# Folding Wq and Wk ahead of the first transposes, one more gelu sum on GpSimd, and new instruction orders in a fused attention and routed-FFN block

## The chip, the cores and the metric

The kernel runs on one NeuronCore of a Trainium2 chip. The metric is device time in microseconds of one execution; lower is better. The kernel before takes 91.41 us, the median of three runs (91.35 to 91.45).

## The reference, cut to what is computed

The input x is 4 x 1024 x 128 in float32. Two sublayers follow each other, each with a layer norm in front and a residual around it.

```python
h = layernorm(x)
q, k, v = heads(h @ Wq + bq), heads(h @ Wk + bk), heads(h @ Wv + bv)   # 16 heads of 8
q, k = elu(q) + 1, elu(k) + 1
k = k / sqrt(sum(k * k) + 1e-6)
attn = (q @ k.T) @ v              # no softmax: computed as q @ (k.T @ v)
y = h + attn @ Wo + bo
x = x + layernorm(y) * gamma + beta
h = layernorm(x)
scores = h @ w_router             # the top 768 of 1024 tokens of each batch are selected
out = h, with gelu(h @ w_block) in the selected rows
x = x + out
```

## The kernel before

The 4096 tokens are 32 tiles of 128 rows. Four tiles make a half u (0 to 7); two halves make a batch b (0 to 3). Every half goes through the same stages, and the halves are interleaved by hand: each engine has one program, a plain list of calls such as `k_half(3)`, and it runs strictly in the order of the list. Engines wait for one another with semaphores. So the order of a list decides what stands behind a wait.

The stages, with the names used in the lists:

- **First norm.** VectorE (DVE) takes statistics (`first_stats`, `bn_x`), GpSimd (POOL) takes the inverse roots with a power operation (`first_roots`, `roots1`), and `normalise1` writes the normalised rows; halves 3 and 7 are normalised on ScalarE (ACT). TensorE (PE) transposes them (`first_transpose`, `transpose_h`), and ACT copies the transposes out of PSUM (`first_copy`, `copy_hT`).
- **Weights.** The biases and the centring of the normalised rows are folded into the weights by two products on PE in `fold_biases`, with `less_last` and `to_last`; `copy_w` (ACT) writes the result to `w_c`. `fold_back` does the like for the residual and bo, into `back`.
- **Queries and keys.** PE: `q_proj`, `k_proj` (`first_keys` for half 0). ACT: `exp_q_half`, `exp_k_half`. DVE: `q_half`, `k_half`. Then the norm of the keys: `square_k` (ACT), `key_sums` (DVE), `ln_norms`, `seed_norms`, `square_seed` (ACT), `key_norms` (DVE), `scale_k` (POOL).
- **Attention.** PE: `attention_matrix(b)`, `values(b)`, `attention_out(b)`, with `copy_hk` and `copy_M` on ACT and `mask_vk(b)` on DVE between them, and `y_half(u)`.
- **Second norm and residual.** `y_stats`, `variances2` (DVE), `roots2` (POOL), `scale_y` and `y_gamma` (DVE), `residual` (DVE; half 0 on POOL), and the statistics of the result, `x1_stats`, `variances3` (DVE), `roots3` (POOL), `affine3` (DVE: two instructions of 128x4).
- **Scores, gelu and merge.** PE: `transpose_x1`, `z_half`. ACT: `gelu`, `norm_sum`. `gelu_sum(u)` adds x1 to the gelu, 128x512; the string `GELU_SUM_BY` says for each half whether POOL or DVE does it. The rank of each token comes from eight comparisons a batch, `compare(b, J)` on DVE, masked by `mask_own`, and summed on PE; `drop_first` and `drop_last` make the flags and `merge(u)` (DVE) puts the rows together. SyncE (SP) stores them. The last half's second part goes out from ACT's queue.

PE starts with `BUSY` products of zeros, before any data has come, so that it is not idle ahead of the first real work. PSUM has eight banks, and `BANK_USES` lists, for each, which result takes it after which; `take` waits until the one before has been read out.

Lines that matter below: L751 `first_stats`, L764 `bn_x`, L773 `normalise1`, L779 `q_half`, L799 and L801 `key_norms`, L813 `mask_vk`, L833 `variances2`, L839 `variances3`, L846 and L847 `affine3`, L853 and L432 `gelu_sum` on DVE and POOL, L886 `residual`, L918 `compare`, L927 `mask_own`, L941 `merge`, L400 `scale_k`, L413 `roots2`, L426 `roots3`, L1152 the zeros, L1165 `first_transpose`, L1197 and L1199 `fold_biases`, L501 `copy_w`, L1174 `first_keys`, L1219 `k_proj`, L1252 `y_half`.

Of the kernel before, what the change touches and what calls it, by code (L numbers as in the profile page):

```python
# [12 lines left out]
P = 128  # L13
# [7 lines left out]
def preln_linear_attention_mod_ffn(nc, x, wq, bq, wk, bk, wv, bv, wo, bo, gamma, beta, w_router, w_block, out):  # L21
# [19 lines left out]
    GELU_SUM_BY = 'PPPPPDDD'  # L41
# [10 lines left out]
    with ExitStack() as ctx:  # L52
# [3 lines left out]
        def sem(name):  # L56
# [6 lines left out]
        hT = sb("hT", [P, U, HW])  # L63
# [40 lines left out]
        w_c = sb("w_c", [P, 3 * P])  # L104
# [11 lines left out]
        back = sb("back", [P, P])  # L116
# [11 lines left out]
        w_in, wo_in, wz_in = sem("w_in"), sem("wo_in"), sem("wz_in")  # L128
# [45 lines left out]
             ("sums", 6),),  # L174
            (("h", 1), ("k", 3), ("M", 0), ("y", 0), ("wz", 0), ("z", 1), ("z", 6), ("xt", 5), ("s", 4),
             ("sums", 3), ("ra", 1), ("ra", 2),),
            (("q", 0), ("q", 4), ("q", 7), ("xt", 1), ("y", 5), ("y", 6), ("sums", 1), ("xt", 7), ("z", 13),),
# [118 lines left out]
        BUSY = 14  # L296
# [29 lines left out]
        def _(pool):  # L326
# [123 lines left out]
            add_beta(3)  # L450
# [1058 lines left out]
```

## Time and profile before

| | us |
|---|---|
| median of the runs (lowest, highest) | 91.41 (91.35, 91.45) |
| the profiled execution | 91.51 |
| its span, first to last instruction | 89.8 |
| PE busy | 79.9 |
| DVE busy | 80.9 |
| ACT busy | 66.9 |
| POOL busy | 52.8 |

The span is what the trace shows. The profiled execution takes 1.71 us more than its span, which lies before the first and after the last instruction. Busy time counts overlapping instructions once; a row's own duration holds the fill and the drain of the engine's pipeline, so instructions that follow each other closely start earlier than the one before ends.

### The profile page before, as it was taken

The page shows a single profiled execution, that of the slowest core. Times are in us where ns is not written, and L with a number is a line of the kernel's source. Part 1 is how long each engine was busy: PE and PEld are TensorE (multiplying, and loading weights), DVE is VectorE, ACT ScalarE, POOL GpSimd, SP SyncE. Part 2 cuts the span into 40 slices and gives each one's busy share as a digit, 9 for nine tenths or more (in the row PEclk, how much of TensorE's full clock was granted, in tenths as well). Part 3 has the DMA queues.
Part 4 walks back from the last instruction along what each step waited for, and adds up shares of the span by engine and source line. Part 5 has one row for each costly group of instructions (what it writes and reads, how often), then busy time and mean ns, then how long its engine had stood idle before and what let it go on. Part 6 is the DMA issues. An engine that isn't in the chain of part 4 may idle for free.

```text
span 89.8 us, 2397 instructions
## 1 busy us (share of the span) xinstructions
PE 79.9 (89%) x816; PEld 68.4 (76%) x816; DVE 80.9 (90%) x258; ACT 66.9 (75%) x186; POOL 52.8 (59%) x79
## 2 busy tenths in 40 slices
PE   4998689999999999999999599999999797999700
PEld 1335656976797997999999599999998797779600
DVE  4368999999797897999999999999999999999960
ACT  5003599998999996753539799999799696998700
POOL 5265885989992997659770979769838400000000
PEclk9999999999999999999999999999999999999996
DMA  0899969970999999900000000000000000348456
GB/s 24 233 256 319 280 168 319 290 189 7 143 127 140 139 143 136 112 10 0 0 0 0 0 7 0 0 4 7 0 4 0 0 7 10 107 121 236 138 149 180
DMA packets 18113, 8.99 MB, mean 100 GB/s; under 512 B 819, under 2 KB 18102, under 8 KB 18102
## 3 DMA queue, kind: packets, MB, share of 16 engines
q1 hardware_dynamic: 13232, 6.49, 26.7%
q0 software_dynamic: 4160, 2.10, 21.5%
q10 hardware_dynamic: 710, 0.26, 1.1%
q8 instruction: 6, 0.10, 0.4%
q14 instruction: 5, 0.04, 0.1%
HBM read 4.66 MB, written 2.10 MB: 75 GB/s over the span
## 4 chain that ended last, share of the span: by engine, by line
PE 46%; DVE 41%; issue 4%; ACT 3%; DVEq 1%; POOL 1%; ACTq 0%
DVE beats L918 11%; PE bank L1219 7%; PE bank L1211 7%; PE bank L1152 6%; DVE xb_sb L886 5%; DVE x_sb L941 5%; DVE bn L893 4%; PE bank L1252 4%; PE bank L1228 4%; PE bank L1253 4%; PE bank L1188 3%; PE bank L1271 3%; DVE beats L927 2%; DVE bn L818 2%; DVE x_sb L853 2%
## 5 line engine op out<-in xcount | busy, mean ns | idle before, releaser
L918 DVE TENSOR_SCALAR beats<-s_row,s_col 128x1024 bf16<-128x1024 f32 (+7 forms) x32 | 15.5, 541 | 0.0
L595 ACT ACTIVATE norm_sb<-xb_sb,shift,gain 128x128 f32<-128x128 f32 x32 | 13.2, 507 | 2.7 <-DVE shift L847 2.7
L1252 PE MATMUL bank<-M_sb,qT 128*128 128x128 f32 x64 | 12.5, 277 | 0.0
L1253 PE MATMUL bank<-back,hT 128*128 128x128 f32 x64 | 12.4, 275 | 0.0
L413 POOL TENSOR_TENSOR r<-var,minus_half 128x4 f32<-128x4 f32 x8 | 8.1, 1025 | 5.8 <-DVE var L833 5.5
L400 POOL TENSOR_TENSOR k_sb<-k_sb,k_rnorm 128x512 f32<-128x512 f32 x8 | 9.3, 1252 | 2.7 <-DVE k_rnorm L801 2.7
L426 POOL TENSOR_TENSOR r<-var,minus_half 128x4 f32<-128x4 f32 x8 | 9.1, 1194 | 2.9 <-DVE var L839 2.9
L1252 PEld LDWEIGHTS bank<-M_sb,qT 128*128 128x128 f32 x64 | 9.7, 192 | 0.2 <-ACT M_sb L558 0.2
L1253 PEld LDWEIGHTS bank<-back,hT 128*128 128x128 f32 x64 | 9.7, 192 | 0.0
L588 ACT ACTIVATE x_sb<-bank,r 128x128 f32<-128x128 f32 x32 | 9.2, 383 | 0.2 <-DVE s_col L901 0.2
L1219 PEld LDWEIGHTS bank<-w_c,hT 128*128 128x128 f32 x56 | 6.9, 192 | 2.1 <-ACT hT L513 1.1
L1271 PE MATMUL bank<-wz_c,hT 128*128 128x129 f32 x64 | 8.5, 278 | 0.0
L1219 PE MATMUL bank<-w_c,hT 128*128 128x128 f32 x56 | 7.3, 277 | 0.9 <-ACT hT L513 0.9
L1211 PE MATMUL bank<-hT,w_c 128*128 128x512 f32 x16 | 8.0, 593 | 0.0
L1228 PE MATMUL bank<-k_sb,norm_sb 128*128 128x128 f32 x64 | 7.8, 275 | 0.0
L1271 PEld LDWEIGHTS bank<-wz_c,hT 128*128 128x128 f32 x64 | 7.7, 192 | 0.0
L886 DVE SCALAR_TENSOR_TENSOR xb_sb<-bank,r,xb_sb 128x128 f32<-128x128 f32 x28 | 7.6, 338 | 0.0
L1228 PEld LDWEIGHTS bank<-k_sb,norm_sb 128*128 128x128 f32 x64 | 7.5, 192 | 0.0
L1292 PE MATMUL bank<-ident,beats 128*128 128x128 bf16 x108 | 6.8, 219 | 0.6 <-DVE dropped L936 0.6
L394 POOL DMA_DIRECT2D xb_sb<-beta_sb x4 | 7.0, 2060 | 0.1
L1152 PE MATMUL bank<-idle 128*128 128x512 bf16 x14 | 5.8, 601 | 1.3 <-DVE idle L735 1.3
L1292 PEld LDWEIGHTS bank<-ident,beats 128*128 128x128 bf16 x108 | 6.2, 98 | 0.9 <-DVE beats L918 0.8
(132 smaller groups left out, 216.7 us busy)
## 6 DMA issues: line engine op xcount, KB each, us to landing
xb_sb<-in_L_attn_x_dram SPq DMA_DIRECT2D x4, 512.0 KB, 6.8
xb_sb<-beta_sb POOLq DMA_DIRECT2D x4, 512.0 KB, 8.4
x_sb<-in_L_attn_x_dram SPq DMA_DIRECT2D x7, 256.0 KB, 5.2
out_dram<-x_sb SPq DMA_DIRECT2D x7, 256.0 KB, 2.3
x_sb<-in_L_attn_x_dram SPq DMA_DIRECT2D x2, 128.0 KB, 2.7
out_dram<-x_sb SPq DMA_DIRECT2D x1, 128.0 KB, 2.4
out_dram<-x_sb ACTq DMA_DIRECT2D x1, 128.0 KB, 2.5
w_sb<-in_L_attn_Wq_dram ACTq DMA_DIRECT2D x1, 64.0 KB, 2.5
```

Source lines behind the costliest of these rows:

```text
L400: nc.gpsimd.tensor_tensor(out_keys, keys, norms, ALU.mult).then_inc(keys_pool, 1)
L595: last = nc.scalar.activation(norm_sb[:, t], xb_sb[:, t], ACT.Identity, bias=shift3[:, t:t + 1], scale=gain3[:, t:t + 1])
L886: last = nc.vector.scalar_tensor_tensor(out=xb_sb[:, n], in0=bank_of(("y", u))[:, t * P:(t + 1) * P], scalar=r2[:, n:n + 1], in1=xb_sb[:, ...
L918: nc.vector.tensor_scalar(beats[:, b % 2, J, P * J:T * P], s_row[:, b, P * J:T * P], s_J, None, ALU.is_le).then_inc(beats_done, 1)
L1152: nc.tensor.matmul(bank[:, 7, :], idle16[:, 0:P], idle16[:], start=True, stop=True)
L1211: nc.tensor.matmul(take(("q", u)), w_c[:, 0:P], hT[:, u], start=True, stop=True).then_inc(q_full, 1)
L1219: last = nc.tensor.matmul(o[:, t * P:(t + 1) * P], hT[:, u, t * P:(t + 1) * P], w_c[:, P:2 * P], start=True, stop=True)
L1228: last = nc.tensor.matmul(o[:, 0:P], norm_sb[:, T * b + t], k_sb[:, 2 * b + t // TH, t % TH], start=(t == 0), stop=(t == T - 1))
L1252: nc.tensor.matmul(o, qT[:, u, t * P:(t + 1) * P], M_sb[:, b], start=True, stop=False)
L1253: last = nc.tensor.matmul(o, hT[:, u, t * P:(t + 1) * P], back[:], start=False, stop=True)
L1271: last = nc.tensor.matmul(o[:, j * (P + 1):(j + 1) * (P + 1)], hT[:, u, t * P:(t + 1) * P], wz_c[:], start=True, stop=True)
L1292: last = nc.tensor.matmul(o[:, n * P:(n + 1) * P], beats[:, b % 2, J, I * P:(I + 1) * P], ident16[:], start=(I == J), stop=(I == T - 1))
```

## The change

- **Fold.** `fold_biases` folds only Wq and Wk (256 columns in place of 384), and stands in front of `first_transpose(0)`. It waits for two weights and two biases. Wv and its bias have semaphores of their own, `wv_in` and `bv_in`, and are folded by two products of 128 columns in `fold_back`. `back` holds both results, `copy_back` copies 256 columns, and `values` reads Wv from it and waits for it for batch 0.
- **Queues.** The load of Wv on SP's queue goes out behind the load of half 1 of x instead of ahead of it.
- **Zeros.** `BUSY` is 10 in place of 14.
- **Gelu sums.** `GELU_SUM_BY` gives `gelu_sum(5)` to POOL, which then has six of eight.
- **Orders.** The lists of POOL, ACT, DVE and PE and the table of banks are new. No operation other than those above is added or left out.

```diff
-    GELU_SUM_BY = 'PPPPPDDD'
+    GELU_SUM_BY = 'PPPPPPDD'
-        BUSY = 14
+        BUSY = 10
@@ sync
                         sp.dma_start(x_sb[:, t:t + TH // 2, :], x_v[b, :, t:t + TH // 2, :]).then_inc(x0_in[h], 16)
-                    sp.dma_start(w_sb[:, 2 * P:3 * P], wv).then_inc(w_in, 16)
                 else:
                     sp.dma_start(x_sb[:, TH * u:TH * u + TH, :], x_v[b, :, a:a + TH, :]).then_inc(x_in[u], 16)
+                if u == 1:
+                    sp.dma_start(w_sb[:, 2 * P:3 * P], wv).then_inc(wv_in, 16)
@@ gpsimd, the list from scale_k(4)
             scale_k(4)
             roots2(0)
             scale_k(5)
+            residual(0)
             roots2(1)
-            residual(0)
+            add_beta(3)
             scale_k(6)
-            scale_k(7)
+            roots3(0)
             roots2(2)
             roots2(3)
-            roots3(0)
             roots3(1)
+            scale_k(7)
             roots2(4)
+            roots3(2)
             roots2(5)
             gelu_sum(0)
             gelu_sum(1)
-            roots3(2)
             roots3(3)
             roots3(4)
             roots2(6)
...
             roots3(5)
             roots3(6)
+            roots3(7)
             gelu_sum(4)
-            roots3(7)
+            gelu_sum(5)
@@ scalar, the first calls
+            copy_w()
             first_copy(0)
-            copy_w()
             first_copy(1)
             exp_k_half(0)
+            exp_q_half(0)
             copy_hT(1)
+            square_k(0)
             normalise1(3)
-            square_k(0)
             exp_k_half(1)
             copy_hT(2)
-            exp_q_half(0)
             copy_hT(3)
@@ vector, the first calls
             normalise1(1)
+            k_half(0)
             bn_x(4)
+            shifts1(2)
             bn_x(5)
-            shifts1(2)
-            k_half(0)
             normalise1(2)
             bn_x(6)
             bn_x(7)
+            k_half(1)
             normalise1(4)
-            k_half(1)
-            normalise1(5)
+            q_half(0)
             key_sums(0)
             key_sums(1)
-            q_half(0)
+            shifts1(4)
+            normalise1(5)
+            k_half(2)
+            q_half(1)
             normalise1(6)
@@ vector, around batch 0's comparisons, the list after
             variances2(5)
             score_cols(1, 0)
             score_cols(1, 1)
             residual(4)
             affine3(1)
             y_gamma(5)
             affine3(2)
             x1_stats(4)
             variances3(3)
             mask_vk(3)
             residual(5)
             compare(0, 0, 1)
...
@@ vector, the end of batch 2's comparisons, the list after
             compare(2, 5, 1)
             drop_last(0)
             affine3(6)
             variances3(7)
             compare(2, 6, 1)
             compare(2, 7, 1)
             drop_first(1)
             mask_own(2, 1)
             gelu_sum(6)
             merge(0)
             affine3(7)
             drop_last(1)
             score_cols(7, 0)
             score_cols(7, 1)
             merge(1)
             merge(2)
             merge(3)
             compare(3, 4, 1)
...
@@ tensor
-                o = take(("wp", 0))[:, 0:3 * P]
-                nc.tensor.matmul(o, less_last[:], w_sb[:], start=True, stop=False)
-                pe.wait_ge(bias_in, 16 * 3)
-                nc.tensor.matmul(o, to_last[:], bias_rows[:], start=False, stop=True).then_inc(w_full, 1)
+                o = take(("wp", 0))[:, 0:2 * P]
+                nc.tensor.matmul(o, less_last[:], w_sb[:, 0:2 * P], start=True, stop=False)
+                pe.wait_ge(bias_in, 16 * 2)
+                nc.tensor.matmul(o, to_last[:], bias_rows[:, 0:2 * P], start=False, stop=True).then_inc(w_full, 1)
@@ fold_back
-                nc.tensor.matmul(take(("rp", 0))[:, 0:P], less_bo[:], centre[:], start=True, stop=True).then_inc(back_full, 1)
+                o = take(("rp", 0))
+                nc.tensor.matmul(o[:, 0:P], less_bo[:], centre[:], start=True, stop=True)
+                pe.wait_ge(wv_in, 16)
+                nc.tensor.matmul(o[:, P:2 * P], less_last[:], w_sb[:, 2 * P:3 * P], start=True, stop=False)
+                pe.wait_ge(bv_in, 16)
+                nc.tensor.matmul(o[:, P:2 * P], to_last[:], bias_rows[:, 2 * P:3 * P], start=False, stop=True).then_inc(back_full, 1)
@@ tensor, the first calls
             busy_start()
+            fold_biases()
             first_transpose(0)
-            fold_biases()
             first_transpose(1)
             first_keys(0)
             first_keys(1)
+            q_proj(0)
             transpose_h(1)
             k_proj(1)
-            q_proj(0)
+            q_proj(1)
             transpose_h(2)
             transpose_h(3)
-            q_proj(1)
-            transpose_h(4)
             k_proj(2)
             k_proj(3)
+            transpose_h(4)
+            q_proj(2)
+            q_proj(3)
+            q_proj(4)
             transpose_h(5)
-            q_proj(2)
+            fold_back()
             k_proj(4)
-            q_proj(3)
             k_proj(5)
```

## Rows read from the trace of the kernel before

**Rows 1.** The page, first part: busy time, share of the span, instructions.
```profile
PE 79.9 (89%) x816; PEld 68.4 (76%) x816; DVE 80.9 (90%) x258; ACT 66.9 (75%) x186; POOL 52.8 (59%) x79
```

**Rows 2.** DVE's timeline, its waits from 5.7 us on: start, duration, instruction, wait.
```profile
5.95 0.76 DVE L764 BATCH_NORM_STATS2 bn<-x_sb 128x6 f32<-128x256 f32 x2 [0.24 <-DMA x_sb<-in_L_attn_x_dram]
...
23.97 0.69 DVE L779 SCALAR_TENSOR_TENSOR qT<-exp_q,bank 128x512 f32<-128x512 f32 x1 [0.57 <-ACT exp_q L521]
...
27.63 0.29 DVE L813 TENSOR_TENSOR vk_sb<-bank,head_mask 128x128 f32<-128x128 f32 x1 [0.47 <-PE bank L1234]
...
31.22 0.29 DVE L799 SCALAR_TENSOR_TENSOR k_tmp<-k_ssq,k_tmp 128x128 f32<-128x128 f32 x1 [0.40 <-ACT k_tmp L550]
...
35.12 0.29 DVE L813 TENSOR_TENSOR vk_sb<-bank,head_mask 128x128 f32<-128x128 f32 x1 [0.49 <-PE bank L1234]
```

**Rows 3.** The timeline's end: DVE's last merges.
```profile
85.43 1.39 DVE L941 COPY_PREDICATED x_sb<-dropped,norm_sb 128x512 f32<-128x512 int32 x3
```

**Rows 4.** The timeline of the first 12 us: zeros, fold, first keys, SP's load.
```profile
1.26 5.76 PE L1152 MATMUL bank<-idle 128*128 128x512 bf16 x14 [1.26 <-DVE idle L735]
...
1.79 0.46 SPq L308 DMA_DIRECT2D w_sb<-in_L_attn_Wv_dram  x1
...
6.86 0.38 PE L1165 MATMUL bank<-ident,norm_sb 128*128 128x128 f32 x2
...
7.08 0.81 PE L1197 MATMUL bank<-w_sb,less_last 128*128 128x384 f32 x2
...
8.57 0.48 ACT L501 COPY w_c<-bank 128x384 f32<-128x384 f32 x1 [0.92 <-PE bank L1199]
...
8.89 1.10 DVE L773 TENSOR_SCALAR norm_sb<-x_sb,bn,r 128x127 f32<-128x127 f32 x4
...
11.64 1.16 PE L1219 MATMUL bank<-w_c,hT 128*128 128x128 f32 x8 [0.88 <-ACT hT L513]
```

**Rows 5.** The timeline: the normalisation of half 5, and the start of `y_half(0)`.
```profile
15.86 1.23 DVE L773 TENSOR_SCALAR norm_sb<-x_sb,bn,r 128x127 f32<-128x127 f32 x4
...
29.33 0.39 PE L1252 MATMUL bank<-M_sb,qT 128*128 128x128 f32 x2
```

**Rows 6.** Groups by line: busy time and mean duration of `gelu_sum` on DVE and POOL.
```profile
L853 DVE TENSOR_TENSOR x_sb<-x_sb,xb_sb 128x512 f32<-128x512 f32 x3 | 1.9, 673 | 0.0
...
L432 POOL TENSOR_TENSOR x_sb<-x_sb,xb_sb 128x512 f32<-128x512 f32 x5 | 6.5, 1302 | 0.5 <-ACT x_sb L588 0.5
```

**Rows 7.** The timeline and groups: DVE instructions beside long POOL instructions on SBUF.
```profile
32.95 0.32 DVE L833 TENSOR_SCALAR var<-y_sq 128x4 f32<-128x4 f32 x1
...
39.94 2.11 POOL L400 TENSOR_TENSOR k_sb<-k_sb,k_rnorm 128x512 f32<-128x512 f32 x2 [1.09 <-DVE k_rnorm L801]
...
41.30 0.76 DVE L833 TENSOR_SCALAR var<-y_sq 128x4 f32<-128x4 f32 x1
...
67.76 1.42 POOL L432 TENSOR_TENSOR x_sb<-x_sb,xb_sb 128x512 f32<-128x512 f32 x1
...
67.98 1.29 DVE L918 TENSOR_SCALAR beats<-s_row,s_col 128x128 bf16<-128x128 f32 x1
...
L833 DVE TENSOR_SCALAR var<-bn 128x4 f32<-128x4 f32 x4 | 0.5, 157 | 0.0
```

**Rows 8.** The timeline: a comparison beside a power operation of POOL.
```profile
54.21 1.08 POOL L426 TENSOR_TENSOR r<-var,minus_half 128x4 f32<-128x4 f32 x1
...
54.50 0.75 DVE L918 TENSOR_SCALAR beats<-s_row,s_col 128x1024 bf16<-128x1024 f32 x1
```

**Rows 9.** The timeline around `gelu_sum(0)`: roots on POOL, residuals and an affine on DVE.
```profile
49.28 1.98 POOL L413 TENSOR_TENSOR r<-var,minus_half 128x4 f32<-128x4 f32 x2 [2.70 <-DVE var L833]
...
50.63 2.15 DVE L886 SCALAR_TENSOR_TENSOR xb_sb<-bank,r,xb_sb 128x128 f32<-128x128 f32 x8
...
52.70 0.16 DVE L846 TENSOR_SCALAR gain<-r 128x4 f32<-128x4 f32 x1
...
52.99 1.28 POOL L432 TENSOR_TENSOR x_sb<-x_sb,xb_sb 128x512 f32<-128x512 f32 x1 [0.48 <-ACT x_sb L588]
```

More of the change, by code:

```diff
@@ L683, in _ @@
             copy_xT(3)
+            norm_sum(2)
+            gelu(2, 0)
+            y_stats(7)
+            copy_s_row(2)
             copy_xT(4)
-            norm_sum(2)
-            y_stats(7)
-            gelu(2, 0)
+            copy_xT(5)
             gelu(2, 1)
@@ L1026, in _ @@
             residual(3)
-            affine3(0)
+            x1_stats(2)
+            y_stats(4)
+            variances3(2)
+            variances2(4)
+            y_stats(5)
+            y_gamma(4)
             score_cols(0, 0)
-            y_stats(4)
-            x1_stats(2)
             x1_stats(3)
-            y_stats(5)
             score_cols(0, 1)
-            variances2(4)
             variances2(5)
@@ L1037, in _ @@
             score_cols(1, 1)
-            variances3(2)
-            y_gamma(4)
+            residual(4)
+            affine3(1)
             y_gamma(5)
-            residual(4)
+            affine3(2)
+            x1_stats(4)
+            variances3(3)
+            mask_vk(3)
             residual(5)
-            affine3(1)
-            mask_vk(3)
-            x1_stats(4)
-            x1_stats(5)
-            variances3(3)
-            variances3(4)
             compare(0, 0, 1)
@@ L1051, in _ @@
             compare(0, 2, 1)
-            affine3(2)
             compare(0, 3, 1)
+            variances3(4)
+            score_cols(2, 0)
+            mask_own(0, 0)
             compare(0, 4, 1)
             compare(0, 5, 1)
-            mask_own(0, 0)
-            variances3(5)
-            y_stats(6)
-            score_cols(2, 0)
-            variances2(6)
             score_cols(2, 1)
             compare(0, 6, 1)
+            affine3(3)
             compare(0, 7, 1)
+            y_stats(6)
+            x1_stats(5)
+            variances2(6)
+            mask_own(0, 1)
+            variances2(7)
             score_cols(3, 0)
-            variances2(7)
             y_gamma(6)
+            variances3(5)
+            y_gamma(7)
             score_cols(3, 1)
-            y_gamma(7)
-            mask_own(0, 1)
-            score_cols(4, 0)
-            score_cols(4, 1)
             residual(6)
@@ L1087, in _ @@
             compare(1, 7, 1)
-            x1_stats(7)
-            drop_last(0)
-            affine3(4)
-            variances3(7)
             score_cols(6, 0)
-            affine3(5)
-            affine3(6)
+            mask_own(1, 1)
             compare(2, 0, 1)
-            mask_own(1, 1)
             compare(2, 1, 1)
+            drop_first(0)
             compare(2, 2, 1)
             compare(2, 3, 1)
+            score_cols(6, 1)
             compare(2, 4, 1)
+            mask_own(2, 0)
             compare(2, 5, 1)
+            drop_last(0)
+            affine3(6)
+            variances3(7)
             compare(2, 6, 1)
             compare(2, 7, 1)
-            score_cols(6, 1)
-            drop_first(0)
+            drop_first(1)
+            mask_own(2, 1)
+            gelu_sum(6)
+            merge(0)
+            affine3(7)
+            drop_last(1)
             score_cols(7, 0)
             score_cols(7, 1)
-            merge(0)
-            mask_own(2, 0)
-            mask_own(2, 1)
-            drop_last(1)
-            gelu_sum(5)
-            drop_first(1)
+            merge(1)
+            merge(2)
+            merge(3)
             compare(3, 4, 1)
@@ L1252, in y_half @@
                     nc.tensor.matmul(o, qT[:, u, t * P:(t + 1) * P], M_sb[:, b], start=True, stop=False)
-                    last = nc.tensor.matmul(o, hT[:, u, t * P:(t + 1) * P], back[:], start=False, stop=True)
+                    last = nc.tensor.matmul(o, hT[:, u, t * P:(t + 1) * P], back[:, 0:P], start=False, stop=True)
                 last.then_inc(y_full, 1)
@@ L1399, in _ @@
             values(1)
+            centre_wz()
             q_proj(7)
@@ L1410, in _ @@
             y_half(4)
+            y_half(5)
+            transpose_x1(2)
             z_half(0, 0)
             z_half(0, 1)
-            y_half(5)
             z_half(1, 0)
```

225 lines of the change are left out of this document (107 added, 118 removed), and 24 rows, old and new, of the table BANK_USES.

## The prediction

> **What bounds the kernel now.** I read the page first. Its first part says that DVE is busy 80.9 us of 89.8, more than any other engine [rows 1]. PE is as good as level with it, 79.9 us, and shares of busy time do not tell who sets the end, so I went to DVE's timeline and listed its waits. After 5.95 us there are four, 0.57 us at 23.4, 0.47 at 27.2, 0.40 at 30.8 and 0.49 at 34.6, together 1.93 us; from 35.12 us to the last merge at 86.82 (85.43 + 1.39) DVE waits for nobody [rows 2, 3]. The reader is to see a queue that is simply full: between 5.95 and 86.82 lie 80.87 us, of which 1.93 are waits. What comes behind the last merge is a store. So a faster step on PE or ACT is worth something only where it takes away one of those four waits, and every instruction taken from DVE is worth its whole time.
>
> One more thing in DVE's time is not work. The last comparison of batch 1, 128 columns, lasts 1.29 us, beside a POOL `gelu_sum` from 67.76 to 69.18, and ends at 69.27, right behind it. `variances2` of 128x4 lasts 0.76 us at 41.30 beside the second of two `scale_k`, and ends at 42.06 when POOL's ends at 42.05; the same operation elsewhere has a mean of 157 ns [rows 7]. So some DVE instructions stand still until a long POOL instruction on SBUF is through. A power operation of POOL does not do that: a comparison of 1024 columns takes 0.75 us beside one [rows 8]. The stalls at 41.30 and 67.98 cost 0.60 and about 1.02 us (1.29 less some 0.27 for 128 columns, an estimate from 0.75 for 1024 and 0.16 for 4); a third, 0.32 us at 32.95, is 0.16 us over the mean [rows 7]. That makes 1.8 us in all.
>
> **The change, part by part.**
>
> *The gelu sum.* One 128x512 addition leaves DVE. Its mean is 673 ns, of which some 0.60 is start to start; POOL takes 1.30 us for it [rows 6] and is busy 52.8 us of 89.8 [rows 1]. Gain 0.60.
>
> *SP's queue.* Wv goes out behind half 1 of x. Its issue takes 0.46 us [rows 4], so half 1 can arrive up to that much earlier, and DVE waits for it 0.24 us [rows 2]. Bounds 0 and 0.24. Later waits for ACT and PE may eat part of it; I take half, 0.12.
>
> *Zeros and fold.* The fourteen zeros take 5.76 us from 1.26 us on, and the first transpose starts at 6.86 [rows 4]. That is 0.41 us for each, or nearly 512 columns at the 1.2 GHz level (0.427), though the column of the granted clock reads 1.00 there; the last one ran at 2.4 GHz, as do the two transposes and the fold at 7.08 (two instructions of 384 columns in 0.81 us, fill and drain included). So 13 x 0.427 + 0.21 = 5.76, and PE's clock rose near 6.5 us. With ten zeros PE is free at 1.26 + 10 x 0.427 = 5.5 us. The fold's first product of 256 columns then takes about 0.86 us at the low level (0.64 for 384 columns without the fill, times 256/384, times 2), the second ends at about 6.9. `copy_w` starts near 7.1 instead of 8.57, 1.5 us earlier. If PE stays at the low level for both products and the two transposes it is 7.5 instead. Neither reaches DVE: half 1 is normalised from 8.89 to 9.99 us because DVE has been busy since 5.95, and PE can't transpose it before. The gap that opens on PE takes `q_proj(0)`. `k_proj(1)`, at 11.64 us before because ACT had `exp_k_half(0)` ahead of the copy, moves to about 11.3 [rows 4]. Moving Wv's two products costs PE nothing in sum (2 x 128 columns later for 2 x 128 sooner). Gain of this part on the end: 0 by itself, 0.3 us of lead for PE; the bound above is the four waits, 1.93 us, the one below is no loss.
>
> *The front of the lists.* Here work is only moved. DVE now does `k_half(0)`, `k_half(1)`, `q_half(0)` and two key sums ahead of `normalise1(5)`, which moves from 15.86 us to about 18.0 [rows 5]. Behind it wait `transpose_h(5)`, `fold_back` and `k_proj(4)` in PE's list. I followed PE's list with the durations of before: it loses about 0.45 us waiting for `copy_hT(2)` and 0.4 for `scale_k(1)`, has done `q_proj(0)` early (0.87), carries 0.44 more of Wv, and comes to `y_half(0)` at 29.3 to 29.4 us, against 29.33 [rows 5]. So the lead is spent, and the train of y halves runs at its old times. DVE's waits move: the one for `exp_q` goes, but with `square_k(5)` late on ACT and `key_sums(5)` behind it the wait for the norms of batch 2 grows from 0.40 to about 1.0; `mask_vk(1)` has 0.45, `key_sums(5)` 0.25, `y_stats(3)` 0.2. That is 1.9 to 1.95 us against 1.93. Cost 0.02, bounds -1.5 and +1.0.
>
> *Stalls beside POOL.* The one at 41.30 goes, since `variances2(1)` now comes with POOL at roots or a residual just ending. The one at 67.98 goes as well: `gelu_sum(4)` moves behind `roots3(7)`, past all comparisons of batch 1. Gain 1.8. New ones come. `gelu_sum(0)` needs `roots2(5)`, 1.0 us behind `variances2(5)` [rows 9], so it starts about 1.1 us behind it. On DVE `affine3(1)` comes 1.25 us behind `variances2(5)` (a residual is half of 2.15, so 1.04 start to start, and two score columns), `affine3(2)` a further 0.75, `variances3(3)` a further 0.8. Two gelu sums of 1.28 back to back cover 1.1 to 3.7 us. Before, `affine3(1)` fell at 52.70, in the 0.48 us that POOL waited between the two sums [rows 9]. If the first affine meets the first sum it waits 1.15, the second then 0.55: 1.7. If it slips ahead, 0.65 and 0.5. If ACT's gelu is late by a microsecond, 0.55. I take 1.4. At the end `gelu_sum(4)` starts about 1.2 us behind `variances3(7)`, and `affine3(7)` 2.1 behind it meets it: 0.36. Together 1.76 against 1.8: gain 0.04.
>
> *The tail.* After `mask_own(3, 0)` DVE has a gelu sum and a merge, 1.2 us, before it needs a flag, and the last affine no longer holds ACT's copy of the last sums. I put no wait here.
>
> **Sum.** 0.60 + 0.12 - 0.02 + 0.04 = 0.74 us less. From the profiled execution's 91.51 us that is 90.77. The median of the runs is 91.41, 0.10 less, so 90.7 us is forecast.
>
> **Rivals.**
>
> *A, the forecast:* 90.7, with 90.2 to 91.2 as its own range. Chance 0.40.
>
> *B, the sums miss the small instructions.* Then 1.4 of the stalls aren't paid: 90.67 - 1.4 = 89.3; with half of them missed 90.0. For it: the affine and `gelu_sum(0)` are within 0.15 us of each other in my reckoning, and before the affine fell in a gap. Against it: the two sums fill 2.6 us without a gap and three such instructions fall in them. Chance 0.18.
>
> *C, slower: two more gelu sums beside merges.* `gelu_sum(4)` and `(5)` now run while DVE does `gelu_sum(6)`, `merge(0)` and `merge(1)`. Before, no DVE instruction with two full operands in SBUF ran beside a 128x512 instruction of POOL, so the trace doesn't price it. Bounds: nothing, or each sum held against DVE in full, 2 x 1.30 [rows 6], of which 0.36 is in the forecast: 90.67 + 2.2 = 92.9; with one of them 91.8. It decides from 0.75 us on. For it: the comparison of 128 columns waited out a whole sum [rows 7]. Against it: that comparison is another kind, with one operand. Chance 0.22.
> The Trainium skill ("SBUF — State Buffer", "Who interferes with whom") says that a DVE instruction with two inputs in SBUF contends with a GpSimd instruction that reads SBUF, and that the loser stands still for the whole instruction. By that rule this rival holds. With the comparison and the power operation of [rows 8] the trace does not agree to the rule in its plain form, since that one reads SBUF too and held nobody; with the two stalls of [rows 7] it agrees.
>
> *D, slower: the front starves PE.* `normalise1(5)` and `(6)` are 2 us and 1.5 us later; my reckoning leaves 0.1 us between being on time and not. If `attention_matrix(0)` slips by 1 us, every y half slips with it and the waits at `key_norms(2)`, `mask_vk(1)` and `y_stats(3)` take it over: 91.7. It decides from 0.7 us on. Chance 0.14.
>
> *E, nothing to be measured:* waits, stalls and the sum cancel, 91.4. Chance 0.06.
>
> **How the numbers follow.** A measurement of this kernel tells 0.2% or 0.18 us from no change. Faster by more: B, and A but for a fifth of it, 0.18 + 0.33 = 0.51. Same: E and 0.06 of A, 0.12. Slower: C, D and the rest, 0.37. The range reaches down to B with somewhat less than all stalls missed, 89.5, and up to nearly all of C, 92.7; outside lie about 0.1 below and 0.1 above.
>
> **What would show it.** `copy_w` near 7.1 us with 256 columns. `y_half(0)` within 0.3 us of 29.33. DVE's waits from 5.7 us on summing to 1.6 to 2.3. One of L846, L847 or `variances3` well over 0.16 us beside POOL's first two gelu sums, and none of the comparisons of batch 1. L853 or L941 over 1 us at the end would be C. `y_half(0)` over 30 us would be D. The forecast is wrong if the stalls sum to under 1 or over 3 us, or if DVE's waits do.

## The result, and the profile after

The changed kernel takes 94.05 us (median of 6 runs, 93.75 to 94.34) against 91.33 us for the kernel before on the same chip (6 runs, 91.03 to 91.45). The ratio is 1.029, with a 95% interval of 1.026 to 1.032: slower by 2.6 us. The forecast was 90.7 us, in a range from 89.5 to 92.7. The profiled execution took 93.77 us with a span of 92.0, that of before 91.51 with 89.8, so the two traces differ by 2.26 us and can be set against each other. Some executions of some kernels below come out more than 1.5% above the others, at a lower granted clock: the medians and ranges given hold every execution, the ratios leave those out.

TensorE's clock is no rival for the difference. The row of 7 to 88 us, of before and of the changed kernel, has the granted clock at 1.00 both times (third number from the end):

```profile
7.00:88.00 81.00, 74.18 (x803) 66.14 (x801) 77.37 (x245) 65.65 (x185) 49.22 (x62) 1.00 0.49 93
7.00:88.00 81.00, 73.78 (x800) 65.71 (x800) 78.59 (x240) 65.42 (x183) 51.06 (x62) 1.00 0.46 86
```

The first part of the page, where [rows 1] stand for before:

```profile
PE 79.1 (86%) x816; PEld 68.2 (74%) x816; DVE 83.3 (91%) x257; ACT 67.4 (73%) x186; POOL 54.9 (60%) x80
```

DVE has one instruction less than before and is busy 2.4 us longer. An engine that does less and is busy longer has instructions that stand still. The groups by line show which (busy us, mean ns of one):

```profile
L849 DVE TENSOR_SCALAR gain<-r 128x4 f32<-128x4 f32 x8 | 3.9, 489 | 0.0
...
L944 DVE COPY_PREDICATED x_sb<-dropped,norm_sb 128x512 f32<-128x512 int32 (+1 forms) x9 | 6.7, 782 | 0.1
...
L434 POOL TENSOR_TENSOR x_sb<-x_sb,xb_sb 128x512 f32<-128x512 f32 x6 | 8.2, 1390 | 0.0
```

The gain of an affine step, four numbers in each partition, has a mean of 159 ns in the kernel before (L846 there) and 489 here. DVE's timeline about POOL's first two gelu sums, where [rows 9] stand for before:

```profile
50.91 1.27 DVE L849 TENSOR_SCALAR gain<-r 128x4 f32<-128x4 f32 x1
...
52.78 0.64 DVE L849 TENSOR_SCALAR gain<-r 128x4 f32<-128x4 f32 x1
```

and POOL's beside it:

```profile
50.89 2.49 POOL L434 TENSOR_TENSOR x_sb<-x_sb,xb_sb 128x512 f32<-128x512 f32 x2
```

The sums run from 50.89 to 53.38 us. `affine3(1)` starts 0.02 us behind the first and ends at 52.18; between it and the next affine lies `y_gamma`, whose source and result are in PSUM and which takes its usual 0.68; `affine3(2)` then ends at 53.42, with the second sum. Against 0.16 us these two cost 1.11 and 0.48. DVE's timeline about the last two sums:

```profile
74.69 0.16 DVE L842 TENSOR_SCALAR var<-bn 128x4 f32<-128x4 f32 x1
...
75.68 0.68 DVE L856 TENSOR_TENSOR x_sb<-x_sb,xb_sb 128x512 f32<-128x512 f32 x1
76.28 1.79 DVE L944 COPY_PREDICATED x_sb<-dropped,norm_sb 128x512 f32<-128x512 int32 x1
77.97 1.22 DVE L849 TENSOR_SCALAR gain<-r 128x4 f32<-128x4 f32 x1
...
88.28 0.78 DVE L944 COPY_PREDICATED x_sb<-dropped,norm_sb 128x256 f32<-128x256 int32 x2
```

and POOL's:

```profile
75.94 3.22 POOL L434 TENSOR_TENSOR x_sb<-x_sb,xb_sb 128x512 f32<-128x512 f32 x2
```

The two sums start 1.25 us behind `variances3(7)` (74.69), just as the prediction reckoned, and take 3.22 us where the first two took 2.49: POOL itself takes longer beside DVE's own gelu sum and merge. The merge at 76.28 takes 1.79 us where 0.73 is usual, and `affine3(7)` behind it 1.22. Together that is 2.12 us. The last merge ends at 89.06, 2.24 us later than before [rows 3].

The front shows in these lines of DVE, PE and ACT, to be held against [rows 2, 4, 5]:

```profile
5.64 0.75 DVE L767 BATCH_NORM_STATS2 bn<-x_sb 128x6 f32<-128x256 f32 x2
...
7.54 0.76 DVE L767 BATCH_NORM_STATS2 bn<-x_sb 128x6 f32<-128x256 f32 x2 [0.64 <-DMA x_sb<-in_L_attn_x_dram]
8.48 0.76 DVE L767 BATCH_NORM_STATS2 bn<-x_sb 128x6 f32<-128x256 f32 x2 [0.17 <-DMA x_sb<-in_L_attn_x_dram]
...
5.27 0.59 PE L1199 MATMUL bank<-w_sb,less_last 128*128 128x256 f32 x2
...
6.33 0.37 ACT L504 COPY w_c<-bank 128x256 f32<-128x256 f32 x1 [4.25 <-PE bank L1201]
...
29.42 0.39 PE L1262 MATMUL bank<-M_sb,qT 128*128 128x128 f32 x2
```

Half 1 of x is there 0.3 us earlier, and half 2 holds DVE up for 0.64 and 0.17 us; `y_half(0)` starts at 29.42 us, against 29.33 before and 29.3 to 29.4 forecast.

The changed kernel also has smaller stalls in its first half, in lines of DVE that usually read 0.16 us for one `variances` step, 0.28 for a key norm (L802) and 1.10 for four normalising steps:

```profile
20.22 1.59 DVE L776 TENSOR_SCALAR norm_sb<-x_sb,bn,r 128x127 f32<-128x127 f32 x4
21.41 0.41 DVE L802 SCALAR_TENSOR_TENSOR k_tmp<-k_ssq,k_tmp 128x128 f32<-128x128 f32 x1
...
36.16 0.53 DVE L836 TENSOR_SCALAR var<-y_sq 128x4 f32<-128x4 f32 x1
...
40.89 0.47 DVE L842 TENSOR_SCALAR var<-bn 128x4 f32<-128x4 f32 x2
```

The first two stand beside POOL's issue of a load (`add_beta(0)`, 20.02 to 21.77 us) and cost some 0.3 us from start to start, the third beside its `residual(0)` (35.39 to 36.67), the fourth beside a `scale_k` (40.20 to 41.27).

To see all of it I added up DVE's time from each start to the next, with the lowest fifth of each kind of instruction as its usual price. From first statistics to the last instruction's start, before and after:

| | before | after |
|---|---|---|
| first `bn_x` starts | 5.95 | 5.64 |
| usual price of all that follows | 75.74 | 74.92 |
| instructions held beside POOL | 1.63 | 4.69 |
| gaps over 0.12 us | 2.42 | 2.55 |
| the rest | 0.64 | 0.83 |
| last instruction starts | 86.38 | 88.63 |

The first line falls by 0.3 us, the second by 0.82, of which the gelu sum is 0.60; the fourth and fifth grow by 0.13 and 0.19. The third grows by 3.06 us, which is more than the whole loss. How the sum is split depends on where the usual price and the limit for "held" are set. The work is the same but for the one gelu sum, so 0.22 of the 0.82 is this uncertainty, and other limits put the growth of the third line at 2.4 to 3.0 us. By each of them it is larger than the 2.24 us by which the last merge is later.

### The profile page after: what moved, and what is told of

Same layout as the page of the kernel before. It is cut to its first block, busy times and chain, and to the rows that moved or that the text cites. A ratio compares the mean times of both kernels' runs of the same rounds, so it can differ in the third digit from the quotient of the medians.

```text
span 92.0 us, 2399 instructions
## 1 busy us (share of the span) xinstructions
PE 79.1 (86%) x816; PEld 68.2 (74%) x816; DVE 83.3 (91%) x257; ACT 67.4 (73%) x186; POOL 54.9 (60%) x80
## 4 chain that ended last, share of the span: by engine, by line
DVE 47%; PE 23%; issue 7%; DMA 6%; ACT 5%; POOL 5%; SPq 2%; DVEq 1%; ACTq 0%
DVE beats L921 14%; DVE xb_sb L889 8%; PE bank L1227 6%; DMA x_sb<-in_L_attn_x_dram 6%; DVE bn L896 5%; POOL r L415 5%; PE bank L1219 5%; PE bank L1236 4%; DVE gain L849 4%; DVE x_sb L944 3%; PE bank L1190 3%; DVE bn L821 2%; PE bank L1263 2%; PE bank L1262 2%; ACT norm_sb L494 2%
## 5 line engine op out<-in xcount | busy, mean ns | idle before, releaser
L428 POOL TENSOR_TENSOR r<-var,minus_half 128x4 f32<-128x4 f32 x8 | 9.5, 1192 | 9.7 <-DVE var L842 9.4
L921 DVE TENSOR_SCALAR beats<-s_row,s_col 128x1024 bf16<-128x1024 f32 (+7 forms) x32 | 15.0, 511 | 0.0
L402 POOL TENSOR_TENSOR k_sb<-k_sb,k_rnorm 128x512 f32<-128x512 f32 x8 | 8.5, 1072 | 3.5 <-DVE k_rnorm L804 3.5
L415 POOL TENSOR_TENSOR r<-var,minus_half 128x4 f32<-128x4 f32 x8 | 8.2, 1027 | 3.8 <-DVE var L836 3.6
L1281 PE MATMUL bank<-wz_c,hT 128*128 128x129 f32 x64 | 9.2, 280 | 0.0
L434 POOL TENSOR_TENSOR x_sb<-x_sb,xb_sb 128x512 f32<-128x512 f32 x6 | 8.2, 1390 | 0.0
L944 DVE COPY_PREDICATED x_sb<-dropped,norm_sb 128x512 f32<-128x512 int32 (+1 forms) x9 | 6.7, 782 | 0.1
```

The lines of the kernel that those rows point to most:

```text
L415: nc.gpsimd.tensor_tensor(r2[:, t0:t1], var2[:, t0:t1], minus_half[:].to_broadcast([P, TH]), ALU.pow).then_inc(r2_done, 1)
L921: nc.vector.tensor_scalar(beats[:, b % 2, J, P * J:T * P], s_row[:, b, P * J:T * P], s_J, None, ALU.is_le).then_inc(beats_done, 1)
L1281: last = nc.tensor.matmul(o[:, j * (P + 1):(j + 1) * (P + 1)], hT[:, u, t * P:(t + 1) * P], wz_c[:], start=True, stop=True)
```

## The experiments

**One small order in the middle.** `affine3(1)` and `(2)` go in front of `residual(4)`, so that they are through before POOL's first gelu sum.

```diff
-            residual(4)
             affine3(1)
-            y_gamma(5)
             affine3(2)
+            residual(4)
+            y_gamma(5)
```

> The changed kernel with two calls of VectorE's list moved: affine3(1) and affine3(2) stand in front of residual(4), so that they run before GpSimd's gelu_sum(0) starts, instead of 1.0 and 2.9 us behind it. Nothing else differs. Theory L (a two-port or two-input VectorE instruction stands still until a 128x512 GpSimd instruction on SBUF is through): the stalls of 1.11 and 0.48 us at L849 go and no other comes in their place but perhaps one at variances3(3), so about 1.6 us less than the changed kernel, 92.5 us, at worst 93.0. Rival W (the changed kernel is slow because its new orders make engines wait for one another, and the long L849 rows only show such waits): the wait moves to the next instruction and the time stays at 94.0 within 0.3.

Measured: 93.24 us (93.01 to 94.08, 4 runs), ratio 1.021 (1.015 to 1.028), about 0.7 us less than the changed kernel, where the intervals of the two ratios allow anything from nearly nothing to 1.3. Theory L had 1.6 less. DVE's timeline of this kernel about the first two sums, which run from 51.02 to 53.51:

```profile
50.17 0.16 DVE L849 TENSOR_SCALAR gain<-r 128x4 f32<-128x4 f32 x1
...
51.95 0.74 DVE L896 BATCH_NORM_STATS2 bn<-xb_sb 128x6 f32<-128x256 f32 x2
52.62 0.92 DVE L842 TENSOR_SCALAR var<-bn 128x4 f32<-128x4 f32 x1
```

The affines cost nothing now, the statistics of x1 beside the sum take their usual 0.74, and `variances3(3)`, another 128x4 instruction, stands until the second sum ends (0.77 us over). A stall that is taken from one instruction falls to the next that can be held. In the trace 0.82 of the 1.59 us came back. The profiled execution shows even less, 93.43 us against 93.77, and its trace has a loss that the changed kernel's has not: its granted clock was 0.50 from 80.9 to 84.2 us, where the changed kernel's was 1.00, and DVE waited 0.38 us for PE at 87.12.

**Fewer sums on POOL at the end.** The changed kernel with `gelu_sum(5)` on DVE, and with `(4)` and `(5)` on DVE.

```diff
-    GELU_SUM_BY = 'PPPPPPDD'
+    GELU_SUM_BY = 'PPPPPDDD'
```

(and `'PPPPDDDD'` in the second; the sums go in front of `gelu_sum(6)` in DVE's list.)

> The changed kernel with gelu_sum(5) given back to VectorE, right in front of its gelu_sum(6); GpSimd keeps gelu_sum(4). VectorE has 0.60 us more to do. Theory L: one of the two stalls of about 1.06 us behind 76 us goes, the other stays (it moves to whichever VectorE instruction comes next, a gelu sum or a merge), so 0.4 to 0.5 us less, 93.6 us. If only one-input instructions in the two-port form could be held, a gelu sum and a merge would not be: then the change would cost 0.6 less 0.36, 94.3 us. Rival W: 0.6 us more, 94.6 us.

> The changed kernel with gelu_sum(4) and gelu_sum(5) both on VectorE in front of its gelu_sum(6); GpSimd does four of eight. VectorE has 1.20 us more to do. Theory L: both stalls behind 76 us go, 2.1 us, so about 0.9 us less than the changed kernel, 93.1 us, with no VectorE instruction over 0.8 us behind 70 us. Rival W: 1.2 us more, 95.2 us.

Measured: 93.48 us (92.85 to 94.78, 4 runs), ratio 1.020 (1.014 to 1.026), and 92.96 us (92.41 to 93.24, 4 runs), ratio 1.016 (1.011 to 1.021). Both are near what theory L says (93.6 and 93.1) and far from rival W (94.6 and 95.2). With one sum left on POOL one stall is left, and it has changed its victim; here two of DVE's own gelu sums, usually 1.28 us together, with POOL's sum from 75.92 to 77.47:

```profile
75.66 2.36 DVE L855 TENSOR_TENSOR x_sb<-x_sb,xb_sb 128x512 f32<-128x512 f32 x2
77.94 0.71 DVE L943 COPY_PREDICATED x_sb<-dropped,norm_sb 128x512 f32<-128x512 int32 x1
```

With none left, no DVE instruction behind 70 us is held. So a sum that DVE does itself costs 0.60 us, and one that POOL does there costs DVE 1.06: giving POOL two more sums in this place is a loss of 0.9, measured as 1.1 us between the changed kernel and the second of these.

**The price of meeting, by itself.** A small kernel runs four DVE instructions of one kind alone, and then beside four POOL additions of 128x512 (its output is only a copy of x), for ten kinds; then five of the kinds beside the issue of a load on GpSimd's queue.

> A kernel that measures by itself which VectorE instructions are held beside GpSimd. It computes nothing of the reference (the output is a copy of x). For each of ten forms VectorE runs the instruction four times alone, then four times from the moment on at which GpSimd starts four 128x512 additions in SBUF; five of the forms are run once more beside a software-queue load of 512 KB issued by GpSimd. Theory L: the comparison (128 columns, bf16 out), the 128x4 scale, the fp32 scale of 128 columns, the 128x127 normalisation, the addition, the bf16 product and the predicated copy are held until the GpSimd addition is through, so their longest row is their time alone plus 0.9 to 1.3 us; the product of a PSUM and an SBUF operand, the statistics and the reduction are not held. Rival P (only one-operand instructions in the two-port form are held): the addition, the product and the predicated copy keep their time alone. Beside the load by the software queue, Theory L: the normalisation is longer than alone by 0.1 to 0.4 us, as at 20.5 us in the changed kernel; by the rival it is not.

The timeline of some kinds, alone and then beside POOL's additions (start, duration of all four):

```profile
10.16 0.87 DVE L109 TENSOR_SCALAR o_compare<-a,col 128x128 bf16<-128x128 f32 x4
12.89 5.01 DVE L109 TENSOR_SCALAR o_compare<-a,col 128x128 bf16<-128x128 f32 x4 [1.86 <-POOL small L74]
17.84 0.38 DVE L111 TENSOR_SCALAR o_var<-a 128x4 f32<-128x4 f32 x4
18.42 2.50 DVE L111 TENSOR_SCALAR o_var<-a 128x4 f32<-128x4 f32 x4 [0.19 <-POOL small L74]
...
32.64 2.54 DVE L115 COPY_PREDICATED o_pick<-flags,a 128x512 f32<-128x512 int32 x4
35.37 6.79 DVE L115 COPY_PREDICATED o_pick<-flags,a 128x512 f32<-128x512 int32 x4 [0.19 <-POOL small L74]
42.05 2.46 DVE L117 SCALAR_TENSOR_TENSOR o_psum<-a,bank 128x512 f32<-128x512 f32 x4
44.70 2.48 DVE L117 SCALAR_TENSOR_TENSOR o_psum<-a,bank 128x512 f32<-128x512 f32 x4 [0.19 <-POOL small L74]
49.60 1.42 DVE L119 BATCH_NORM_STATS2 o_stats<-a 128x6 f32<-128x256 f32 x4 [2.41 <-POOL pc L77]
51.21 1.42 DVE L119 BATCH_NORM_STATS2 o_stats<-a 128x6 f32<-128x256 f32 x4 [0.19 <-POOL small L74]
```

There are two classes and nothing between. Comparisons, 128x4 arithmetic, scaling (0.87 to 4.92), normalising (1.10 to 4.92), masking in bf16 (1.43 to 5.67), additions (2.50 to 6.74) and merges all wait out POOL's additions. An operation with one of its two operands in PSUM, the statistics, and a reduction (2.47 and 2.46) don't notice them. POOL's side, four additions alone with the statistics and four beside DVE's additions:

```profile
25.90 6.26 POOL L77 TENSOR_TENSOR pc<-pa,pb 128x512 f32<-128x512 f32 x4
...
51.13 4.92 POOL L77 TENSOR_TENSOR pc<-pa,pb 128x512 f32<-128x512 f32 x4
```

POOL loses time too, though less: its four additions take 6.26 us beside DVE's additions, 6.28 beside merges and 5.46 beside the bf16 masks, and 4.91 to 4.93 beside all other kinds. The kinds that cost POOL something have two full operands in SBUF and are also longer than the other held ones, so this kernel doesn't tell which of the two decides. It fits the 3.22 us of the changed kernel's last two sums, beside a gelu sum and a merge. Rival P, by which additions and merges keep their time, is refuted. The doubt on which rival C had been given 0.22 (that a comparison is another kind than a merge) is gone: both kinds are of the held class.

**The front alone.** The kernel before with ten zeros, Wq and Wk folded first, Wv's load behind half 1 of x, and its fold with `fold_back`; all orders else as before, and the gelu sums untouched. In the first, `fold_back` comes behind `transpose_h(5)` on PE and its copy behind `exp_q_half(2)` on ACT; in the second, behind `attention_matrix(0)` and `exp_q_half(4)`.

```diff
             busy_start()
-            first_transpose(0)
             fold_biases()
+            first_transpose(0)
             first_transpose(1)
...
             transpose_h(5)
+            fold_back()
```

> The kernel before with only the first part of the change: ten zeros, Wq and Wk folded in front of the first transposes, Wv's load behind half 1 of x and its fold in fold_back (called behind transpose_h(5), its copy behind exp_q_half(2)); all other orders and the gelu sums as before. Theory L: this part is worth nothing by itself, since VectorE is full; 91.3 us within 0.4, with VectorE's waits for half 2 and 3 of x about 0.3 us longer. Rival F (the front is what costs, by the load order or the clock): at least 1 us more than before, 92.3 us or over.

> The same as e4 but with the fold of Wv where the kernel before has its fold_back, between attention_matrix(0) and k_proj(6), and its copy on ScalarE behind exp_q_half(4), so that no projection waits for that copy. In e4 k_proj(4) shared a PSUM bank with the fold and waited 1.13 us for its copy, and the start of y_half(0) moved from 29.33 to 31.01 us. Theory S (a slip of TensorE's train at 29 us passes to the end one for one, and the rest of the front is worth nothing): y_half(0) starts 0.4 to 0.5 us later than before (the two products more of 128 columns, each in two passes) and the time is 91.3 to 91.9 us. Rival F (the earlier fold, the zeros or the load order cost by themselves): 93 us or more, as e4.

Measured: 93.86 us (93.18 to 97.1, 6 runs), ratio 1.024 (1.019 to 1.029, from four of them), and 92.98 us (92.1 to 93.67, 4 runs), ratio 1.009 (1.006 to 1.012, from the two at 92.1 and 92.3). Both expectations were too low, by the ratios some 2.2 us against 91.3 and 0.3 us against the upper end of theory S; the first lies where rival F has it, the second between theory S and rival F. In the first, the place that I had given the copy was a bad one, and `k_proj(4)` waits for it. PE's timeline of the first of the two:

```profile
20.82 1.13 PE L1226 MATMUL bank<-w_c,hT 128*128 128x128 f32 x8 [1.13 <-ACT back L506]
...
31.01 0.39 PE L1261 MATMUL bank<-M_sb,qT 128*128 128x128 f32 x2
```

and of the second:

```profile
30.13 0.39 PE L1261 MATMUL bank<-M_sb,qT 128*128 128x128 f32 x2
```

`y_half(0)` is 1.68 and 0.80 us later than in [rows 5], and DVE's last merge ends 1.68 and 0.80 us later than in [rows 3] (88.49 and 87.62). What PE loses ahead of `y_half(0)` is passed on one to one in both. Of the second's 0.80 us the three products that stand for one account for 0.44; 0.24 was lost before, where PE waited 0.28 us at 15.66 for normalised rows, and the rest at `values`, which now waits for the copy. So the point from which rival D decides is real, and the new front is harmless only with the new orders around it, in which `y_half(0)` slips by 0.09.

**The changed kernel with its stalls taken apart.** The affines early, `variances3(3)` behind `residual(5)`, `gelu_sum(4)` and `(5)` on DVE, `add_beta(0)` behind `scale_k(1)`.

```diff
+            affine3(1)
+            affine3(2)
             residual(4)
-            affine3(1)
             y_gamma(5)
-            affine3(2)
             x1_stats(4)
-            variances3(3)
             mask_vk(3)
             residual(5)
+            variances3(3)
```

> The changed kernel with the collisions taken apart: affine3(1) and affine3(2) in front of residual(4) as in e1, variances3(3) behind residual(5), gelu_sum(4) and gelu_sum(5) on VectorE as in e3, and GpSimd's add_beta(0) behind scale_k(0) and scale_k(1) instead of in front. Theory L: the five stalls of 0.5 to 1.1 us go, for 1.2 us more of work: 94.05 - 1.6 - 0.9 - 0.3 = 91.3 us, within 0.5. If the slowdown had a second cause of about the same size, 92.5 us or more.

Measured: 91.44 us (90.93 to 93.28, 12 runs), ratio 1.000 (0.998 to 1.002), where 91.3 was expected. All 2.6 us are gone, with the new front and all other new orders left in place, and with 1.2 us more of work on DVE. What is held beside POOL falls to 0.61 us.

**The kernel before with its stalls taken apart.** `y_gamma(2)` in front of `variances2(2)`, `gelu_sum(4)` on DVE.

```diff
-    GELU_SUM_BY = 'PPPPPDDD'
+    GELU_SUM_BY = 'PPPPDDDD'
...
-            variances2(2)
             y_gamma(2)
+            variances2(2)
```

> The kernel before with its own two large collisions taken apart: y_gamma(2) in front of variances2(2), so that the latter no longer meets GpSimd's scale_k(7) (0.60 us), and gelu_sum(4) on VectorE behind drop_last(1), so that the comparison of 128 columns at 68 us is not held (1.02 us) for 0.60 us more of work. Theory L: 0.5 + 0.4 = 0.9 us less than before, 90.4 us, and faster than both kernels. If VectorE's stalls are slack that something else takes up: 91.3 us.

Measured: 90.70 us (90.43 to 90.85, 6 runs), ratio 0.991 (0.989 to 0.993), 0.8 us less where 0.9 was expected. This beats both kernels, with two calls of DVE exchanged and the opposite of what the change does to the gelu sums: one fewer on POOL. No instruction from 5.9 us on is held by more than 0.17 us.

**The sixth sum alone.** The kernel before with `'PPPPPPDD'`, `gelu_sum(5)` behind `roots3(7)` on POOL.

```diff
-    GELU_SUM_BY = 'PPPPPDDD'
+    GELU_SUM_BY = 'PPPPPPDD'
...
             roots3(7)
+            gelu_sum(5)
```

> The kernel before with the second part of the change alone: the sixth gelu sum goes to GpSimd behind roots3(7) and leaves VectorE; both front lists, the folds and the zeros stay as before. Forecast's reasoning (a sum taken off VectorE is worth what a gelu sum takes there): 0.60 us less than before, 90.8. Theory (VectorE instructions with two SBUF inputs wait out a GpSimd add of 128x512): the two sums now run in one stretch of about 2.5 us in the last stage, where VectorE works on merges and copies, and hold up one more of them by about 1.06 us: 1.06 less 0.60 = 0.46 us more than before, 91.8. Settled by: one VectorE instruction behind 70 us lengthened by 1 us or more beside the second GpSimd sum, or none.

Measured: 93.85 us (92.19 to 95.09, 10 runs); the ratio, 1.009 (1.005 to 1.012), or 0.8 us slower, is from the three at 92.2 to 92.5. DVE's timeline of it, where 128x896 takes some 0.69 us:

```profile
71.46 1.69 DVE L919 TENSOR_SCALAR beats<-s_row,s_col 128x896 bf16<-128x896 f32 x1
```

beside POOL's sum:

```profile
71.26 1.42 POOL L432 TENSOR_TENSOR x_sb<-x_sb,xb_sb 128x512 f32<-128x512 f32 x1
```

The comparison takes 1.01 us more, as theory says, though the victim is a comparison and no merge, and the two sums of POOL are apart (67.72 and 71.26 us). With 0.60 us less for the sum that makes 0.4 us more on DVE. The profiled execution took 94.01 us, and its trace shows a second loss behind the first. Two rows of its DVE, then the 36 products of one mask sum on PE in it and in the kernel before, then its row of 76.8 to 80.2 us, with the granted clock third from the end:

```profile
77.47 1.27 DVE L919 TENSOR_SCALAR beats<-s_row,s_col 128x512 bf16<-128x512 f32 x4 [0.43 <-ACT s_row L603]
...
83.30 0.16 DVE L932 TENSOR_SCALAR dropped<-bank 128x4 int32<-128x4 f32 x1 [1.42 <-PE bank L1320]
```

```profile
76.66 3.80 PE L1292 MATMUL bank<-ident,beats 128*128 128x128 bf16 x36
```

```profile
75.67 2.17 PE L1292 MATMUL bank<-ident,beats 128*128 128x128 bf16 x36
```

```profile
76.80:80.20 3.40, 3.40 (x36) 3.40 (x34) 2.97 (x10) 2.78 (x9) 0.00 (x0) 0.50 0.26 77
```

PE waited 1.65 us for DVE's score columns ahead of 75.62 us, against 0.63 in the kernel before; then its granted clock was 0.50, the 1.2 GHz level, in the row shown, its products took 3.80 us for 2.17, and DVE waited 0.43 and 1.42 us for what came of them. The kernel before has neither wait, and a granted clock of 1.00 there. That the longer wait let the clock fall is argued, not shown. How much of this is in the executions near 92.2 us, where 0.4 of the 0.8 us is unexplained, isn't shown either.

**Where Wv's load goes.** The changed kernel taken apart, with Wv's load ahead of half 1 of x again; and the same with `y_gamma(1)` in front of `variances2(1)` and `q_half(7)` in front of `variances3(0)`.

```diff
+                    sp.dma_start(w_sb[:, 2 * P:3 * P], wv).then_inc(wv_in, 16)
                 else:
                     sp.dma_start(x_sb[:, TH * u:TH * u + TH, :], x_v[b, :, a:a + TH, :]).then_inc(x_in[u], 16)
-                if u == 1:
-                    sp.dma_start(w_sb[:, 2 * P:3 * P], wv).then_inc(wv_in, 16)
```

> The changed kernel with all stalls taken apart (as in the run that came to 91.44 us), and with Wv's load in front of the second half of x's first loads, as the kernel before has it. If the order of the two loads is what made the second half late (0.64 and 0.17 us of waits on x in the changed kernel), the wait falls to about 0.2 us and the time to 91.1 to 91.3 (0.1 to 0.3 less than the kernel it is made from). Rival: the transfers share the queues in either order, Wv's fold comes later instead and the time stays at 91.4, or rises by up to 0.3.

> The kernel of the run with Wv first, and two small orders changed beside it: y_gamma(1) in front of variances2(1), which stood beside a residual of GpSimd (0.36 us over its usual time), and q_half(7) in front of variances3(0) and (1), of which one stood beside scale_k(6) (0.25 us over). Theory (even the 128x4 instructions wait for GpSimd): up to 0.6 us less than the kernel with Wv first, if the instruction that comes into the place of each is one that is not held: 90.7 to 90.9. Rival: the place of the stall only moves to the next instruction (q_half and y_gamma have f32 sources in SBUF too), and the time stays within 0.2 us.

Measured: 91.15 us (90.92 to 91.45, 12 runs), ratio 0.997 (0.994 to 0.999), against 1.000 (0.998 to 1.002) without the first edit; and 90.77 us (90.56 to 91.66, 12 runs), ratio 0.993 (0.990 to 0.996). Both are where they were expected, but each step is only just as large as the intervals can tell. DVE's statistics of half 2 in the first of them:

```profile
6.03 0.76 DVE L764 BATCH_NORM_STATS2 bn<-x_sb 128x6 f32<-128x256 f32 x2
...
7.20 0.76 DVE L764 BATCH_NORM_STATS2 bn<-x_sb 128x6 f32<-128x256 f32 x2
```

Half 1 is 0.4 us later than in the kernel it is made from (5.62), and half 2, at 7.20 instead of 7.62 us, 0.4 earlier. Half 2 counts, since DVE had to wait for it. In the second, what is held falls from 0.61 to 0.13 us, and the time by 0.38.

## Why the prediction was wrong

Its steps, in their order:

- **The bound** was right for both kernels. In the changed one too DVE's last wait over 0.2 us ends at 31.02 us, and its sum from start to start closes to the last instruction. It doesn't hold for every kernel here: with the sixth sum alone DVE waited 1.42 us for PE at 83.30.
- **The gelu sum, -0.60:** right as a price of the work. The usual price of DVE's work fell by 0.82, this sum being 0.60 of it and the rest what the method can't resolve.
- **Zeros and fold, 0:** right on the end, wrong in a detail. `copy_w` started at 6.33 us and not near 7.1, because PE's products already ran at the 2.4 GHz level at 5.27 (0.43 us for 256 columns, where 0.86 was taken). It made no difference: in the changed kernel taken apart, whose first fold product took 0.86, `y_half(0)` started at 29.26.
- **SP's queue, -0.12:** the 0.3 us that half 1 gained was lost again on half 2 (0.64 and 0.17 us of waits, which the prediction did not look for). Undoing it gained 0.34% (1.000 to 0.997), so the order by itself cost some 0.3 us, with an interval that reaches from nearly 0 to 0.6. As far as that tells, the term had the wrong sign; its two bounds, 0 and -0.24, left a loss out without a reason.
- **The front lists, +0.02:** right in sum, and partly by luck. Gaps are 2.55 us against 2.42, `y_half(0)` is 0.09 later. The wait for the norms of batch 2 grew to 1.12 us, where 1.0 was forecast. But of the 0.45, 0.25 and 0.2 us forecast at `mask_vk(1)`, `key_sums(5)` and `y_stats(3)` only 0.13 at `key_sums(5)` is there, and the 0.81 us of waits for x, which weren't forecast, stand in their place.
- **Old stalls, -1.8:** all three went, the two at 41.30 and 67.98 as said. But `variances2(1)`, which was to find POOL at roots, met `residual(0)` at 36.16 and took 0.53 us, 0.37 over, `variances3(0)` or `(1)` met `scale_k(6)` at 40.89 (0.25), and a normalising step and a key norm beside `add_beta(0)` cost 0.3. The list of what POOL does next to whom was made for the old stalls only.
- **New stalls in the middle, +1.4:** right, measured 1.59.
- **New stalls at the end, +0.36:** this is the step that failed, and with it the chance of 0.22 for rival C. Measured 2.12: one whole sum against a merge, one against `affine3(7)`. The prediction had the sums' start right, 1.2 us behind `variances3(7)`. It then priced only the affine, by what would be left of the first sum, and put the merge down as possibly of another kind. The merge met the first sum and pushed the affine into the second. The runs show that a merge is not of another kind, and that the class which is not held is that with an operand in PSUM, the statistics and the reductions.
- **The tail, 0:** right. DVE has no wait over 0.12 us there.

The forecast had DVE 0.74 us earlier at the end, and it is 2.24 later, 2.98 apart. Of these 1.76 are the two stalls at the end (2.12 less 0.36), 0.92 the small ones of the first half (0.37, 0.25, 0.3), 0.19 the middle, and 0.1 what is left, front and loads together. This is also why the time lies above the range's upper end, which was rival C without the small ones.

[Rows 7] could have been read as a rule and not as three events: DVE instructions of two kinds, one of them on four numbers in each partition, stood until a POOL instruction with its operands in SBUF was through. The rival's section of the Trainium skill ("SBUF — State Buffer", "Who interferes with whom") goes on beyond the sentence that the prediction used. It says that DVE's tensor_scalar forms too can take the port pair that DVE shares with GpSimd, that tensor_reduce never does, and that a DVE instruction with one input in SBUF outside such modes does not contend. The small kernel agrees on each: 0.87 to 4.92, 2.47 to 2.46, and 2.46 to 2.48 us. It also says that an instruction with two SBUF inputs contends, and the addition agrees (2.50 to 6.74). For the merge, which the section does not name, the run decides: 2.54 to 6.79. I had weighed against the rule that POOL's power operation holds nobody [rows 8]. That is so, but it is a difference between POOL's operations, seen beside a comparison with one full operand, and says nothing about a merge.

## What to carry to other kernels

Work that goes from a full VectorE to an idle GpSimd is worth the time that VectorE spent on it less what its GpSimd version holds up there. Here 0.60 us came off, and what went on was the part of the addition that was left when a held instruction came, however short that was: 1.0 to 1.1 us for those that came near its start, 0.48 and 0.77 for later ones. It pays only where VectorE works on PSUM, on statistics or on reductions for as long as it lasts. List for every long GpSimd instruction which VectorE instructions of the held class fall into it, after the change and not only before; and if one is moved out of the way, ask which comes next. Look also at who waits for VectorE behind the stall: in the kernel with the sixth sum alone TensorE waited 1.65 us instead of 0.63, and VectorE waited 1.85 us in all behind that, though that the one led to the other isn't shown.

Where loads share a queue, look at the wait for each piece, not only for the first: a load put off behind piece 1 is in front of piece 2.

## What the runs showed of the hardware

- A VectorE instruction on 4 numbers in each partition can take 1.27 us instead of 0.16, since it waits for the end of a GpSimd addition (52.18 and 52.16 us in the changed kernel). In the kernel of its own, four of them between them waited out two additions of 1.23 us and were done at 2.50.
- The issue of a load on GpSimd's queue lengthens some of the same instructions, but little: beside it four comparisons took 1.08 us instead of 0.87 and four normalising steps 1.49 instead of 1.10, while additions (2.50), merges (2.55) and bf16 masks (1.43) kept their times.
- TensorE's clock rises at another moment in each trace, under the same zeros. Ten zeros of 512 columns took 3.90 us in one trace and 4.45 in another, fourteen 5.08 to 6.15; the fold's first product of 256 columns took from 0.43 to 0.86. The level is read from these durations, since the column of the granted clock reads 1.00 from the start. The times of the first 7 us of PE should not be compared to 0.5 us between two traces.
- It needn't fall alike either. In the changed kernel PE waited 1.75 us for DVE ahead of 79.51 us, and the granted clock stayed at 1.00 until 88 us. With the affines early it waited the same 1.75 us ahead of 78.83, and the granted clock was 0.50 from 80.9 to 84.2 us.
